# Moving one PSUM copy from ScalarE to VectorE, with the order of all steps set anew, in a six-layer attention and gated-MLP kernel

## What is computed

```python
def layer(h, p):                        # 16 heads of 8 channels
    q, k = h @ wq.T + bq_, h @ wk.T + bk_
    scores = einsum('blhd,bmhd->bhlm', q, k) / sqrt(8)
    w_avg = softmax(scores, -1).mean(axis=1)          # mean over the heads
    new_w = softmax(w_avg + rel, -1)                  # rel: exp(-|i-j|/16)
    h1 = ln(h + new_w @ h, l1w, l1b)
    h2 = ln(h1, l2w, l2b)
    ff = relu(h2 @ w1.T + b1) @ w2.T + b2
    return ln(h2 + ff, l3w, l3b)                      # the third normalisation
x = x + scan(layer, layernorm(x))                     # 6 layers
h = silu(y @ w1) * (y @ w2); h = gelu(h @ h1); h = gelu(h @ h2); x = x + h @ w3   # y = layernorm(x)
```

## Time and profile before

| what | value |
|---|---|
| median of 3 runs | 2712.04 us |
| the profiled execution: its own time | 2713.88 us |
| its span, first to last instruction | 2712.1 us |
| mean granted TensorE clock | 0.995 |
| busy: TensorE, VectorE, ScalarE, GpSimd | 2537.1, 2452.9, 2440.3, 1433.3 us |

### The profile page before, as it was taken

How to read it: one execution, slowest core, us unless ns; L and a number is a source line. 1 busy time by engine, 2 the same in 40 slices (tenths; PEclk the granted TensorE clock), 3 DMA queues, 4 the chain that set the end, 5 groups by cost and what they waited for, 6 DMA issues and landing times.

```text
span 2712.1 us, 88896 instructions
## 1 busy us (share of the span) xinstructions
PE 2537.1 (94%) x35336; PEld 1213.4 (45%) x35336; DVE 2452.9 (90%) x5616; ACT 2440.3 (90%) x6799; POOL 1433.3 (53%) x1564
## 2 busy tenths in 40 slices
PE   5899999999999999999999999999999999988999
PEld 1344444444444444444444444444444443446777
DVE  5999999999999999999999999999999999963333
ACT  4999999999999999999999999999999999962222
POOL 3467755565565564655656556556566555544000
PEclk8999999999999999999999999999999999999999
DMA  4122222211222112122121122111221211100000
GB/s 129 48 79 72 68 72 69 64 47 51 68 66 60 53 53 64 51 68 64 53 59 50 53 81 72 50 59 53 61 62 53 68 45 55 50 14 17 16 16 24
DMA packets 98912, 152.86 MB, mean 56 GB/s; under 512 B 17856, under 2 KB 81088, under 8 KB 88896
## 3 DMA queue, kind: packets, MB, share of 16 engines
q1 hardware_dynamic: 97872, 145.99, 17.6%
q10 hardware_dynamic: 624, 1.18, 0.1%
HBM read 92.58 MB, written 41.94 MB: 50 GB/s over the span
## 4 chain that ended last, share of the span: by engine, by line
ACT 37%; DVE 34%; PE 19%; issue 10%; POOL 1%; ACTq 0%; DMA 0%; SPq 0%; POOLq 0%; DVEq 0%
ACT ex L866 32%; DVE negmax L689 24%; PE m L1005 4%; PE mean L1093 3%; PE sc L1093 3%; PE mean L1016 3%; PE sc L998 2%; DVE pt L700 2%; DVE bn L653 2%; ACT ew L872 2%; ACT relu L917 2%; DVE mv L644 1%; DVE veps L648 1%; PE m L1024 1%; PE m L1105 1%
## 5 line engine op out<-in xcount | busy, mean ns | idle before, releaser
L866 ACT ACTIVATE ex<-sc,negmax 128x512 f32<-128x512 f32 x3072 | 2136.4, 829 | 16.2 <-DVE negmax L689 14.7
L689 DVE TENSOR_REDUCE negmax<-sc 128x1 f32<-128x512 f32 x3072 | 1926.4, 676 | 30.7 <-PE sc L998 15.5
L998 PE MATMUL sc<-kb,qb 96*32 96x512 bf16 x12288 | 1062.0, 384 | 99.3 <-ACT ex L866 92.8
L866 ACT ACTIVATION_READ_ACCUMULATOR ex<-sc,negmax 128x1 f32 x3072 | 1069.9, 348 | 0.0
L1016 PE MATMUL mean<-ex,rw 128*32 128x512 f32 x6144 | 803.8, 594 | 7.5 <-ACT ew L872 7.5
L998 PEld LDWEIGHTS sc<-kb,qb 96*32 96x32 bf16 x12288 | 331.4, 94 | 974.8 <-ACT ex L866 844.3
L511 POOL TENSOR_TENSOR rw<-sel_sb,zinv 128x256 f32<-128x256 f32 x384 | 236.2, 616 | 617.7 <-DVE zinv L695 617.7
L1016 PEld LDWEIGHTS mean<-ex,rw 128*32 128x32 f32 x6144 | 199.5, 110 | 157.1 <-issue 80.5
L1005 PE MATMUL m<-hc,pt 128*32 128x129 f32 x6144 | 206.0, 274 | 6.2 <-DVE pt L700 0.8
L1005 PE MATMUL m<-h2t,w_sb 128*32 128x512 f32 x1536 | 204.7, 597 | 5.5 <-ACT relu L917 2.7
L483 POOL TENSOR_TENSOR rstd<-veps,nhalf 128x4 f32<-128x4 f32 x160 | 163.2, 1020 | 76.8 <-DVE veps L650 56.0
(11 more groups left out here) (111 smaller groups left out, 2455.1 us busy)
## 6 DMA issues: line engine op xcount, KB each, us to landing
kb<-qk_split SPq DMA_DIRECT2D x288, 128.0 KB
qb<-qk_split SPq DMA_DIRECT2D x564, 64.0 KB
qk_split<-kp SPq DMA_DIRECT2D x144, 128.0 KB, 1.9
qk_split<-qp SPq DMA_DIRECT2D x141, 128.0 KB, 1.8
hc<-hs SPq DMA_DIRECT2D x48, 256.0 KB, 2.7
xin<-x SPq DMA_DIRECT2D x16, 256.0 KB, 2.7
fh_raw<-fh SPq DMA_DIRECT2D x2, 1024.0 KB, 5.3
y_kept<-xin SPq DMA_DIRECT2D x8, 256.0 KB, 2.0
```

The costliest lines, as they stand in the source:

```text
L689: nc.vector.tensor_reduce(negmax[:, s % RT:s % RT + 1], sc[s % NS][:, :], AX, ALU.max, negate=True) \
L866: nc.scalar.activation(ex[:, s % ET, :], sc[s % NS][:, :], ACT.Exp, bias=negmax[:, c:c + 1], accum_out=zsum[:, c:c + 1]).then_inc(exp_read ...
L998: ins = nc.tensor.matmul(sc[s % NS][h * QS:h * QS + QS, :], qb[t % 2][:, h % 2, g, h // 2, r:r + QS], kb[t % 2][:, g, h // 2, :], start=Tr ...
```

## The change

The copy of the turned rows moves from ScalarE (`activation` with Copy) to VectorE (`tensor_copy`), from slot 189 to slot 191, and 44 of the lines of `STEP` get other numbers. The sequence of the code inside a slot stays; the new VectorE step stands between `spread` 2 and `queries`. Nothing is added or removed otherwise. Of the table the lines below are those of which the prediction speaks (the others, of the MLP among them, move in the same way).

```diff
-    "invert_sums": (12, 18, 26, 37, 42, 52, 58, 66),
+    "invert_sums": (10, 19, 25, 37, 42, 52, 60, 65),
-    "residual": (40, 61, 76, 82),
-    "stats0": (66, 76, 77, 83),
+    "residual": (40, 60, 76, 81),
+    "stats0": (72, 75, 82, 83),
     "spread": (83, 95, 175),
...
-    "relu": (146, 150, 153, 158),
+    "relu": (145, 150, 153, 157),
...
-    "norm3_out": (189,),
+    "norm3_out": (191,),
...
-    "project": (194, 199),
-    "queries": (195,),
-    "keys": (197,),
-    "split_q": (223, 223, 226, 233),
-    "split_k": (207, 207, 218, 230),
+    "project": (195, 200),
+    "queries": (197,),
+    "keys": (199,),
+    "split_q": (223, 224, 227, 233),
+    "split_k": (206, 207, 222, 223),
...
@@ block.vector
                     spread(2, t + 1, None)
+                for t in due("norm3_out", 0, g, j):
+                    dve.wait_ge(xh3t_ready, late_input(t) + 1)
+                    nc.vector.tensor_copy(h3t[:, :], m1[:, :]).then_inc(ht_ready, 1)
                 for t in due("queries", 0, g, j):
@@ block.scalar
-                for t in due("norm3_out", 0, g, j):
-                    act.wait_ge(xh3t_ready, late_input(t) + 1)
-                    nc.scalar.activation(h3t[:, :], m1[:, :], ACT.Copy).then_inc(ht_ready, 1)
```

More of the change, by code:

```diff
@@ L45 @@
 STEP = {
-    "invert_sums": (12, 18, 26, 37, 42, 52, 58, 66),
-    "row_weights": (14, 16, 28, 42, 45, 50, 67, 73),
-    "sum_heads": (21, 22, 25, 26, 32, 34, 45, 47, 52, 57, 61, 64, 69, 72, 73, 75),
+    "invert_sums": (10, 19, 25, 37, 42, 52, 60, 65),
+    "row_weights": (14, 16, 30, 41, 42, 53, 67, 69),
+    "sum_heads": (21, 22, 25, 26, 32, 34, 45, 47, 52, 56, 61, 64, 69, 71, 73, 75),
     "exp_mean": (25, 47, 63, 73),
     "transpose_mean": (30, 53, 68, 79),
-    "relative": (35, 56, 73, 78),
-    "attend": (40, 59, 76, 82),
-    "residual": (40, 61, 76, 82),
-    "stats0": (66, 76, 77, 83),
+    "relative": (35, 54, 73, 78),
+    "attend": (40, 59, 76, 81),
+    "residual": (40, 60, 76, 81),
+    "stats0": (72, 75, 82, 83),
     "spread": (83, 95, 175),
[L56 to L59, removed]
+    "power": (89, 99, 179),
+    "apply0": (89, 89),
+    "norm1_weight": (92,),
+    "norm1_bias": (93,),
     "stats1": (94, 94, 94, 94),
-    "apply1": (107, 107),
+    "apply1": (99, 112),
     "norm2_turn": (143,),
@@ L64 @@
     "token_weight": (141,),
-    "token_bias": (143,),
+    "token_bias": (142,),
     "up": (146, 151, 156, 158),
-    "relu": (146, 150, 153, 158),
+    "relu": (145, 150, 153, 157),
     "down": (163, 165, 170, 172),
@@ L70 @@
     "stats2": (173, 174, 174, 174),
-    "apply2": (175, 176),
+    "apply2": (178, 179),
     "norm3_turn": (191,),
-    "norm3_out": (189,),
-    "norm3_weight": (178,),
-    "norm3_bias": (182,),
-    "project": (194, 199),
-    "queries": (195,),
-    "keys": (197,),
-    "split_q": (223, 223, 226, 233),
-    "split_k": (207, 207, 218, 230),
-    "last_weight": (185,),
-    "last_bias": (192,),
+    "norm3_out": (191,),
+    "norm3_weight": (181,),
+    "norm3_bias": (183,),
+    "project": (195, 200),
[3 more added lines that the diff above has]
+    "split_k": (206, 207, 222, 223),
+    "last_weight": (179,),
+    "last_bias": (189,),
     "last_add": (193,),
[L84 to L87, removed]
+    "last_stats": (192,),
+    "last_spread": (194,),
+    "last_power": (203,),
+    "last_apply": (204,),
     "last_turn": (205,),
     "last_keep": (203,),
[L90 to L93, removed]
+    "first_stats": (0, 0, 0, 0),
+    "first_spread": (5,),
+    "first_power": (10,),
+    "first_apply": (12, 44),
     "first_turn": (47,),
     "first_out": (46,),
-    "first_token": (45,),
+    "first_token": (47,),
     "first_project": (51, 55),
@@ L99 @@
     "first_keys": (54,),
[L100 to L109, removed]
+    "first_split_q": (54, 56, 62, 65),
+    "first_split_k": (56, 58, 63, 67),
+    "head_high": (39, 39, 39, 39, 39, 39, 41, 52),
+    "head_low": (43, 43, 43, 49, 53, 60, 63, 66),
+    "head_first": (64, 64, 67, 68, 73, 73, 78, 79),
+    "head_silu": (64, 65, 67, 67, 72, 75, 82, 89),
+    "head_gate": (67, 69, 70, 70, 70, 76, 81, 84),
+    "head_square": (73, 86, 89, 92, 95, 96, 118, 118, 119, 133, 140, 140, 141, 150, 172, 175),
+    "head_gelu": (79, 86, 91, 92, 95, 95, 108, 117, 117, 117, 119, 124, 146, 152, 167, 172),
+    "head_split": (99, 107, 118, 121, 123, 124, 127, 170),
 }
```

## The result

| | median of the runs | range | runs |
|---|---|---|---|
| before | 2712.04 us | 2711.91 to 2713.90 | 5 |
| after | 2742.51 us | 2738.47 to 2754.95 | 5 |

What follows compares the result with a forecast made beforehand. ScalarE was taken as the bound, with VectorE taking over after the change at 48.37 - 0.38 + 0.60 + 0.30 = 48.89 us a unit. The period falls 0.27 us over 36 periods: 2712.0 - 9.8 = 2702.2 us, range 2695 to 2724.

Steps and rivals of the forecast that it cites:

- What bounds the kernel before: Middle units: ScalarE is the bound, busy 48.86 of 49.16 us, with VectorE 0.5 us behind it.
- The stall of `veps` 1: `spread` 1 on VectorE: `veps` slips in after GpSimd's first tensor_tensor, waiting 0.03 us; a gain of 0.38 us a unit.
- the second rival: At `spread` 1, GpSimd's second split gets in before `veps` 1: period 49.87 us, 2737.6 us in all; chance 0.07.
- The stall as long as what is left of GpSimd's instruction: Shared SBUF ports at `veps` 1: whoever starts first holds them for the whole instruction; 0.58 us in the trace agrees.
- The race of `zz`: VectorE's `zz` meets GpSimd's `rw`, which leads by 0.04 to 0.05 us, in every unit; no stall taken.
- The first rival: GpSimd wins the race: `zz` stands 0.44 us behind `rw` in each unit; 2720.7 us; chance 0.36.
- The copy on VectorE: Copy out of PSUM adds 0.60 us a unit to VectorE, 0.66 kept for the range, with no wait ahead.
- The copy off ScalarE: ScalarE loses 0.47 us a unit, from 48.86 to 48.39 us of work.
- The sum: VectorE per middle unit: 48.37 - 0.38 + 0.60 + 0.30 idle = 48.89 us; the period falls by 0.27.
- The third rival: Path shared by ScalarE, TensorE and VectorE: the copy is no relief, period 49.16, 2712 us; chance 0.14.

Runs made afterwards that it cites:

- e2: The kernel before with `power` 1 moved from slot 106 to 98, ahead of a GpSimd CAST; 2706.28 us, ratio 0.9973.
- e1: The kernel after with GpSimd's second split of `qf` moved from slot 224 to 227, behind the `power`, and the third to 228; 2696.96 us, ratio 0.9943.
- e7: e1 with the copy back on ScalarE, so new slots without the copy and without the stall; 2706.24 us, ratio 0.9978.
- e3: The kernel before with only the copy moved to VectorE, in slot 191, all other slots old; 2715.14 us, ratio 1.0009.
- e6: e3 with the edit of e2, so old slots, copy on VectorE and `power` 1 eight slots earlier; 2706.75 us, ratio 0.9979.
- the eight kernels of the table: All combinations of old or new slots, copy on ScalarE or VectorE, with or without the stall, before and after included; medians 2697.0 to 2751.6 us.

## Why the prediction was wrong, step by step

- **What bounds the kernel before: right.** e2 stops at ScalarE's work, 48.81 us in a period of 48.89.
- **The stall of `veps` 1: the step that failed.** The text said that 8.96 holds for its arrival, that the first tensor_tensor ends at 8.97, and that `veps` slips in. GpSimd's chain was right to 0.02 us (the second tensor_tensor begins 8.95 behind `veps` 0). VectorE's was not: 9.03 in all units of the middle, 0.07 later than taken. The 8.96 was read in the last layer of the old order, where the inversion of the sums stands behind seven `negmax`. In the new slots it stands two slots earlier (10 for 12), behind six, and in e1, where nothing else disturbs, VectorE waits 0.44 us for the sums there, 4.2 us behind `veps` 0; shorter distances behind the inversion and behind the four `bn` (by 0.10 and 0.20 us) give part of it back:

```profile
1081.73 3.67 DVE L689 TENSOR_REDUCE negmax<-sc 128x1 f32<-128x512 f32 x6
1085.85 0.20 DVE L695 RECIPROCAL zinv<-zsum 128x8 f32<-128x8 f32 x1 [0.44 <-ACT ex L869]
```

  The prediction carried a number across a stretch whose instructions the diff had put in another order, and gave the other outcome of a margin of 0.01 us only 7%. The margin was not even that: by the 1.12 of the earlier trace rows from one long split to the next the second begins at 7.81 + 1.12 = 8.93, ahead of 8.96, and not at the first one's end of 8.97. A gain of 0.38 became a loss of 0.53 (0.58 to 1.11), and the period went with it. I had the mechanism as the second rival; its period was right within 0.32 us, its chance was not. That its 2737.6 us lie near the measured 2742.5 is luck: the period was taken 0.32 us a unit too long, and the falls were not in it.
- **The stall as long as what is left of GpSimd's instruction: right.** In every case above `veps` waits to the end of the instruction that GpSimd had begun, and not at all for one that begins later. The Trainium skill (SBUF — State Buffer, Who interferes with whom) states it so, and these rows agree (1.11, 0.57, 0.27 and 0.17 us).
- **The clock: a term that was missing.** No case in the text had TensorE slowed. The stall adds 17 falls, 17 us, more than half of the loss. The place could be seen in the profile before: TensorE was busy for 2.27 of 3.40 us there, the thinnest stretch of a unit. That a longer stall would bring the clock down behind it could not.
- **The race of `zz`: no stall, as taken, for a reason that was off.** `zz` takes 0.14 to 0.15 us in all 48 units. But the lead of `rw` that I had worked out, 0.04 to 0.05, is not there. In the timeline after both start together, within 0.01 us in 47 units:

```profile
1702.19 0.19 DVE L695 RECIPROCAL zinv<-zsum 128x8 f32<-128x8 f32 x1
1702.30 0.24 DVE L653 BATCH_NORM_STATS2 bn<-res 128x6 f32<-128x128 f32 x1
1702.46 0.14 DVE L774 SCALAR_TENSOR_TENSOR zz<-res 128x4 f32<-128x4 f32 x1
...
1702.46 0.63 POOL L511 TENSOR_TENSOR rw<-sel_sb,zinv 128x256 f32<-128x256 f32 x1 [0.99 <-DVE zinv L695]
```

  The `bn` comes 0.11 behind the inversion as in the earlier trace rows, but `zz` follows it by 0.16 and not by the 0.21 of the earlier trace rows. The first rival, at 36%, rested on a lead that came from adding up distances of other places.
- **The copy on VectorE: right.** It stands 0.60 us ahead of the next instruction (1686.54 to 1687.14), with no wait ahead:

```profile
1686.54 0.68 DVE L801 COPY h3t<-m 128x512 f32<-128x512 f32 x1
1687.14 1.28 DVE L689 TENSOR_REDUCE negmax<-sc 128x1 f32<-128x512 f32 x2
```

  That is the 0.60 of the `negmax` in the earlier trace rows. The 0.66 that the Trainium skill gives (VectorE: DVE Perf Modes, the TRN2 errata) lies near the record's own duration, 0.68; for the distance to the next instruction, which is what the sum needs, it is 0.06 too much here.
- **The copy off ScalarE: the size was off.** 0.47 us was taken, and ScalarE's busy time falls by 0.33 from e7 to e1 (48.95 to 48.62).
- **The sum.** It took `veps` 1 as nearly free of GpSimd and had a period of 48.89: 48.59 us of VectorE's work and 0.30 of its idle time. e1, which has no stall, has 48.70, with 48.11 of work and 0.59 of idle time, 0.44 of it the wait for the sums. So the sum was near by luck: the work was taken 0.48 too high, as if it were the same in every table of slots, and the idle time 0.29 too low. (The 9.8 us are 36 x 0.27 = 9.7; that changes nothing.)
- **The third rival, that the copy is no relief**, is what happens in the old slots (e3 and e6).

## What stays open

Why the clock falls in 17 units and not in the others is not settled: TensorE is busy for 1.76 to 1.77 us of that stretch in 30 units of the middle, and the clock falls in 14 of them. Nor is it settled why the same instructions of VectorE take 0.49 us less in the new slots: by the distances to the instruction behind (e1 against e6, mean of the 36 periods) the `negmax` take 0.19 us a unit less, the inversions 0.16, the `res` and the `bn` of `h` 0.08 each, so no one place makes it. And how the stall at 9 us thins the stretch at 20 us is read from waits (TensorE for ScalarE for VectorE); that it does is borne out by the eight kernels of the table, in which TensorE's 2.50, 2.28 and 1.8 us go with the three lengths of `veps` 1.

## What to carry to other kernels

Where two engines meet within a tenth of a microsecond in every round of a loop, the outcome is not a detail but a fixed cost in all rounds; reckon the arrival of both from the new order, give both outcomes a real chance, and, better, put between them something that keeps the long GpSimd instruction away from that place: here another order of a few instructions is worth 45 us. Look in each unit for the stretch in which TensorE does least: here a delay that made it thinner cost 17 us of clock on top of the 13 of the delay. And test a move both with and without the rest of the change, for here, without the stall, the copy and the slots are worth nothing apart and 9 us together.

## What was unexpected of the hardware

- The price of a start that came too late by 0.10 us is nearly the whole instruction of the other engine: 1.11 us for an operation of 0.17, behind a GpSimd tensor_tensor of 1.18. With equal starts (`zz` and `rw`, both at 1702.46) VectorE wasn't held, in none of 47 such meetings.
- A granted clock of 0.52 over 3.40 us, with TensorE busy for 1.76 of the 3.40 us ahead of it, costs 1.0 us of a unit. With that stretch filled to 2.88 it didn't occur in any of 36 units, and the redundant matmuls made the kernel 10 us faster.
